# Moving the first expert tile's transposes and first product into the last attention step of a gated-linear-attention and mixture-of-experts kernel

## The chip, the core and the metric

The kernel runs on one core of one Trainium2 chip. The metric is the device time of one execution in microseconds (us), and the times given for a kernel are the median of several executions. The engines are named as in the profile: PE (TensorE, with PEld its weight loads), DVE (VectorE), ACT (ScalarE), POOL (GpSimd) and SP (SyncE, which here only issues transfers).

## The reference, cut to what matters

```python
# attention block; x is (8, 512, 256), two heads of 128 channels
h = layernorm(x)
q, k, v = silu(h @ wq), sigmoid(h @ wk), h @ wv
f = 1 - k                                  # decay of each channel
theta = cumsum(sign(f - 0.5)) * pi         # so cos is +-1, sin is 0
S = S * f + k (x) v ; o = (q * scale) . S  # a scan over 512 tokens
o = layernorm(o * sigmoid(h @ wg1 @ wg2)) * norm_w
x1 = x + o @ wo
# expert block on z = layernorm(x1); 8 experts, 4096 rows
e = argmax(z @ centroids.T) ; alpha = sigmoid(max affinity)
y = z + relu(layernorm(z, ln_g[e], ln_b[e]) @ w1[e].T + b1[e]) @ w2[e].T + b2[e]
out = x1 + alpha * y + (1 - alpha) * z     # rows in their old order
```

## The kernel before

**Attention as a pipeline.** Eight sequences (NSEQ) go through nine steps (`pipeline`, `step(a, b, c, nxt)`). In step i sequence a is projected, b, the one before it, has its scan, and c, two before, has its gated output normed, projected with `wo`, added to x and routed. The order of the instructions on each engine is written out by hand in that engine's `step`. Engines meet by counting semaphores: `need(eng, sem, per, s, k)` makes an engine wait until event k of sequence or tile s has happened. In the last step (i = 8) a is None, b is the last sequence (LAST_SEQ) and c the one before it (LAST_BUT_ONE).

**The scan.** It is a tree of seven levels over each chunk of 128 tokens. For a level and a head, ACT copies the keys that take part (`mix`), PE multiplies them with the queries (`level`, line 978, into one of two banks bank_l), DVE multiplies the decays in (`update`, line 1328) and picks the scores (`pick`, line 1339). The next level waits for these. Behind level 6 come `k_transposes` (line 1043), copies of them by ACT (`k_tok_copies`), `key_values` (line 1056), a short chain on DVE (`states`, lines 1511 and 1519) and `outputs` (lines 1070 and 1071). `output` on DVE gates the result (`gating`, line 1530).

**Routing.** `ranks` (PE) and `slots` (DVE) give each row a place in its expert's region of a DRAM buffer, `scatter_rows` (POOL, line 631) writes the rows there, each with z, x1 + z, alpha and its row number. The tables of the first NA = 12 tiles need only the first five sequences (EARLY); they are made in step 7 (`early_tables`, signals s_idx 1 and 2). The tables of the others are made behind sequence 7 (`last_tables`, s_idx 3 to 5).

**Expert tiles.** 39 tiles of 128 rows, each of one expert. For tile n: POOL fetches its rows (`gather`, line 683) into one of four slots (SLOTS) and SP the expert's w1 of 1 MB (`fetch_w1`, line 531) into one of four; PE transposes the 256 channels (`z_transposes`, line 1203, into bank_b[0]); ACT applies the expert's norm gains (`gains`, line 911, into xl_t, of which there are two); PE makes the first product (`up`, line 1215, 32 matmul records in two banks bank_a); DVE adds b1 (`bias_h`, line 1627); ACT takes the relu (`relu`, line 921); PE makes the second product (`down`, line 1231); DVE finishes (`finish`, lines 1636 and 1641); POOL scatters to the output (`scatter`, line 695). On PE `turn(n)` is up(n+1), z_transposes(n+2), down(n). Tiles from 12 on use `down_in_parts`, and most are in a loop (`rounds`).

**Around the change.** Behind the last step PE does z_transposes 0 and 1, the ranks of sequence 6 (LAST_BUT_ONE), up(0), the transposes of the last sequence's output (line 1087), then turn(0), the projection with wo (line 1094), turn(1), and so on, with the parts of the last sequence's end between turns. On SP the first four w1 fetches come behind the last step's fetch of x_res, which waits for `residual` (DVE, line 1505) of the sequence before. On POOL the four first gathers stand in the last step behind `norm("o", c)` and one `scatter_rows`. The arena is one block of SBUF that both halves of the kernel lay out anew; xl_t and y_sb lie over the level masks, which the last sequence's picks still read.

## Time and profile before

| | |
|---|---|
| median of 3 runs | 609.88 us |
| the three runs | 609.61, 609.88, 614.47 us |
| profiled execution | 613.98 us, its span 612.2 us |
| PE busy | 568.2 us (93% of the span) |
| PE weight loads busy | 490.3 us (80%) |
| DVE, ACT, POOL busy | 432.9, 341.8, 313.1 us |
| mean granted PE clock | 0.982 of full speed |

The span is the time from the first to the last instruction of the profiled execution; 1.8 us lie around it. Busy shares are averages over stages whose limits differ, so a change of one stage is read in that stage's rows. Matmuls are pipelined: a record may begin before the one ahead of it has ended, and the step from one group's start to the next one's is what a group costs.

### The profile page before, as it was taken

How to read it: one execution, taken by the hardware profiler on the slowest of the kernel's cores; microseconds unless marked ns; L12 is line 12 of the kernel's file. 1: busy time of each engine (PE TensorE's matmuls, PEld its weight loads, DVE VectorE, ACT ScalarE, POOL GpSimd, SP SyncE). 2: the span in 40 equal slices, each digit the busy share in tenths (PEclk: the TensorE clock that was granted, in tenths of full speed). 3: DMA queues.
4: the chain of work that ended last, by engine and by line, in shares of the span. 5: the costliest groups of instructions: out<-in, count | busy, mean ns of one | idle time of the engine just before them, and what ended most of it. 6: DMA issues, size and time to landing. Idle time of an engine off the chain costs nothing.

```text
span 612.2 us, 12947 instructions
## 1 busy us (share of the span) xinstructions
PE 568.2 (93%) x3854; PEld 490.3 (80%) x3854; DVE 432.9 (71%) x990; ACT 341.8 (56%) x754; POOL 313.1 (51%) x390
## 2 busy tenths in 40 slices
PE   2988999999999999999779999999999999999991
PEld 1556778687777867777669998999999999999990
DVE  1396895969779597898672445435888888888880
ACT  3464758768586775856564342224565565565550
POOL 7715244564725548253613425335767767767721
PEclk9999999999999999999699999999999999999996
DMA  8920111121112011020469447556765665665400
GB/s 300 417 94 0 35 36 35 70 70 60 46 35 76 30 69 36 13 92 2 124 213 347 168 160 256 190 190 208 231 217 193 225 228 190 239 224 195 142 6 0
DMA packets 25188, 83.61 MB, mean 137 GB/s; under 512 B 3821, under 2 KB 13423, under 8 KB 18992
## 3 DMA queue, kind: packets, MB, share of 16 engines
q1 hardware_dynamic: 16896, 59.57, 27.6%
q0 software_dynamic: 7552, 22.89, 11.4%
q8 instruction: 24, 0.39, 0.3%
q10 hardware_dynamic: 688, 0.52, 0.3%
q14 instruction: 28, 0.23, 0.1%
HBM read 70.35 MB, written 13.53 MB: 137 GB/s over the span
## 4 chain that ended last, share of the span: by engine, by line
PE 81%; DVE 8%; issue 4%; POOL 3%; DMA 2%; ACT 1%; DVEq 0%; ACTq 0%; POOLq 0%
PE bank_a L1215 21%; PE bank_a L990 8%; PE bank_l L978 7%; PE bank_l L1231 6%; PE bank_l L1250 4%; PE bank_l L1245 4%; PE bank_l L1246 4%; PE bank_c L1094 4%; PE bank_a L1019 4%; DVE arena L1328 3%; PE bank_b L1071 3%; PE bank_a L1035 2%; PE bank_a L1028 2%; PE bank_b L1070 2%; PE bank_c L1111 2%
## 5 line engine op out<-in xcount | busy, mean ns | idle before, releaser
L1215 PE MATMUL bank_a<-masks,arena 128*128 128x128 f32 x1248 | 145.9, 275 | 0.0
L1215 PEld LDWEIGHTS bank_a<-masks,arena 128*128 128x128 f32 x1248 | 143.4, 192 | 0.5
L1328 DVE TENSOR_TENSOR arena<-arena 128x256 f32<-128x256 f32 x224 | 92.1, 456 | 12.4 <-PE bank_l L978 11.0
L978 PEld LDWEIGHTS bank_l<-arena,k_mix 128*128 128x128 f32 x448 | 65.2, 197 | 43.7 <-ACT k_mix L732 27.4
L1627 DVE TENSOR_TENSOR arena<-bank_a,b_col 128x512 f32<-128x512 f32 x78 | 53.9, 691 | 63.9 <-PE bank_a L1215 52.7
L683 POOL DMA_INDIRECT arena<-rows_by_expert,take_idx x39 | 47.7, 1223 | 81.7 <-DVE k_mix L1641 79.3
L978 PE MATMUL bank_l<-arena,k_mix 128*128 128x128 f32 x448 | 72.9, 288 | 10.6 <-DVE arena L1339 7.3
L990 PE MATMUL bank_a<-arena 128*128 128x512 f32 x160 | 82.0, 611 | 0.0
L732 ACT ACTIVATE k_mix<-arena 128x128 f32<-128x128 f32 x224 | 60.4, 308 | 35.7 <-DVE arena L1328 30.7
L911 ACT ACTIVATE masks<-bank_b,b_col,g_col 128x128 f32<-128x128 f32 x78 | 31.4, 454 | 60.4 <-PE bank_b L1203 60.4
L1647 DVE TENSOR_TENSOR w_low<-w_sb,w_high 128x2048 fp32r<-128x2048 f32 x27 | 61.9, 2293 | 3.7 <-issue 2.8
L689 POOL TENSOR_SCALAR put_of<-arena,skip 128x1 int32<-128x1 f32 x39 | 61.7, 1583 | 1.0
L921 ACT ACTIVATE h_high<-arena 128x512 fp32r<-128x512 f32 x54 | 31.1, 623 | 53.8 <-PE bank_l L1250 51.2
L657 POOL TENSOR_TENSOR arena<-arena 128x512 f32<-128x512 f32 (+6 forms) x56 | 27.5, 490 | 59.4 <-DVE arena L1489 55.6
L695 POOL DMA_INDIRECT out<-k_mix,put_of x39 | 41.4, 1063 | 24.2 <-DVE k_mix L1641 13.5
L1245 PE MATMUL bank_l<-w_high,h_high 128*128 128x256 f32 x216 | 53.0, 288 | 0.8 <-ACT h_high L921 0.8
L732 ACT ACTIVATE w_high<-w_sb 128x2048 fp32r x27 | 51.2, 1895 | 0.0
L1246 PE MATMUL bank_l<-w_low,h_high 128*128 128x256 f32 x216 | 50.6, 277 | 0.0
L1231 PE MATMUL bank_l<-w_sb,arena 128*128 x192 | 43.7, 381 | 1.3 <-issue 1.3
L732 ACT ACTIVATE arena<-bank_a 128x512 f32<-128x512 f32 x40 | 23.8, 594 | 34.5 <-PE bank_a L1019 28.5
L631 POOL DMA_INDIRECT rows_by_expert<-arena x32 | 33.5, 1048 | 16.6 <-issue 16.6
L1245 PEld LDWEIGHTS bank_l<-w_high,h_high 128*128 128x128 f32 x216 | 40.6, 188 | 1.0 <-issue 1.0
(160 smaller groups left out, 1079.4 us busy)
## 6 DMA issues: line engine op xcount, KB each, us to landing
arena<-w SPq DMA_DIRECT2D x39, 1024.0 KB
arena<-x SPq DMA_DIRECT2D x16, 512.0 KB, 3.5
w_sb<-w SPq DMA_DIRECT2D x8, 1024.0 KB, 14.8
arena<-b SPq DMA_DIRECT2D x1, 1024.0 KB
arena<-rows_by_expert,take_idx POOLq DMA_INDIRECT x39
out<-k_mix,put_of POOLq DMA_INDIRECT x39
rows_by_expert<-arena POOLq DMA_INDIRECT x32
arena<-wk SPq DMA_DIRECT2D x1, 256.0 KB, 4.0
```

The source lines that it names most:

```text
L683: pool.indirect_dma_start(out=gathered[p].bitcast(I32), out_offset=None, in_=rows, in_offset=bass.IndirectOffsetOnAxis(ap=take_idx[:, n:n ...
L689: pool.tensor_scalar(put_of[:, n:n + 1], gathered[p][:, 2 * D + 1:2 * D + 2], skip[:, n:n + 1], None, ALU.add).then_inc(s_put, 1)
L732: return act.activation(dst, src, ACT.Copy)
L978: ins = pe.matmul(bank, k_mix[l % 2][:, m * P:(m + 1) * P], level_queries(buf, m, l), start=True, stop=True)
L990: return pe.matmul(bank[:, :], w[:, i * width + h * P:i * width + (h + 1) * P], xn_t[:, i * T:(i + 1) * T], start=(i == 0), stop=(i == DC ...
L1215: m = pe.matmul(bank_a[k // 4][:, k % 4 * P:(k % 4 + 1) * P], w1_now[t.par][:, i * F + k * P:i * F + (k + 1) * P], xl_t[t.par % 2][:, i * ...
L1231: m = pe.matmul(bank_l[p][:, 0:D], h_act[:, k * P:(k + 1) * P], w2_sb[:, bass.ds(e * (FC * D) + k * D, D)], start=(k == 0), stop=(k == FC ...
L1245: pe.matmul(bank_l[p][:, 0:D], h_high[:, h], w2_high[p][:, w], start=(k == 0), stop=False)
L1246: pe.matmul(bank_l[p][:, 0:D], h_high[:, h], w2_low[p][:, w], start=False, stop=False)
L1328: dve.tensor_tensor(half, half, factor(decay[b.par], h, l, second), ALU.mult).then_inc(s_up, 1)
L1627: dve.tensor_tensor(h_sb[:, n * 512:(n + 1) * 512].rearrange("p (k t) -> p k t", t=P), bank_a[n][:, :].rearrange("p (k t) -> p k t", t=P), ...
L1647: dve.tensor_tensor(w2_low[t.par % 2], w2_of(e), w2_high[t.par % 2], ALU.subtract).then_inc(s_wlo, 1)
```

## The change

Four moves, each with what has to go with it.

1. z_transposes(0) goes into the last step of PE, behind level 3 and the output transposes of c; up(0) follows in the same step, its first half ahead of `k_transposes`, its second half between these and `key_values`. ACT's gains(0) stands behind o_copy, ahead of mix 5, its relu(0) behind x1_copies; DVE's bias_h(0) stands behind `states`. xl_t[0] moves from the masks to a place of its own in the arena.
2. Behind the last step the order of PE becomes z_transposes(1), down(0), ranks, up(1), z_transposes(2), output transposes, turn(1), projection, turn(2) and so on: the parts of the last sequence stand one turn later. ACT, DVE and POOL follow.
3. SP fetches w1 of tile 0 at the start of the last step, then waits for the rows of all four first tiles, then fetches w1 of tiles 1 to 3 and b2; the fetch of x_res comes behind these.
4. POOL's gathers 0 and 1 stand at the head of the last step, 2 and 3 where they all stood; turn(0) comes ahead of `double_norm(LAST_SEQ)`.

```diff
--- before.py
+++ after.py
@@ -182,6 +182,7 @@
...
         gathered = [lay3.take(RW + 2)[:, 0:RW] for _ in range(SLOTS)]
+        xl_0 = lay3.take(DC * P)
         h_sb = lay3.take(F)
@@ -223,8 +224,8 @@
...
         over_masks = masks[:, :].bitcast(F32)
-        xl_t = [over_masks[:, i * DC * P:(i + 1) * DC * P] for i in range(2)]
-        y_sb = over_masks[:, 2 * DC * P:2 * DC * P + D]
+        xl_t = [xl_0, over_masks[:, 0:DC * P]]
+        y_sb = over_masks[:, DC * P:DC * P + D]
         norm_col = sb("norm_col", [P, DC], F32)
@@ -508,10 +509,6 @@
...
                     sp.dma_start(tiles(x_sb[ahead.par]), seq_rows(x_t, ahead)).then_inc(s_x[ahead.par], 16)
-                if b is not None:
-
-                    need_apart(sp, s_x1, 2, b, 0)
-                    sp.dma_start(tiles(x_res), seq_rows(x_t, b)).then_inc(s_xres, 16)
                 if a is None:
@@ -519,8 +516,16 @@
...
                     need(sp, s_q0, 1, b, 1)
-                    for n in range(SLOTS):
+                    fetch_w1(tile(0))
+                    for p in range(SLOTS):
+                        sp.wait_ge(s_rows[p], 16)
+                    for n in range(1, SLOTS):
                         fetch_w1(tile(n))
+                    sp.dma_start(b2_sb, b2.rearrange("e f -> (e f)").partition_broadcast(P)).then_inc(s_b2, 16)
+                if b is not None:
+
+                    need_apart(sp, s_x1, 2, b, 0)
+                    sp.dma_start(tiles(x_res), seq_rows(x_t, b)).then_inc(s_xres, 16)
 
@@ -531,10 +536,9 @@
...
-
-            sp.dma_start(b2_sb, b2.rearrange("e f -> (e f)").partition_broadcast(P)).then_inc(s_b2, 16)
             for n in range(SLOTS, NA):
                 fetch_w1(tile(n))
+            sp.wait_ge(s_idx, 3)
             rounds(sp, fetch_w1)
@@ -632,18 +636,22 @@
...
             def step(a, b, c, nxt):
+                if a is None:
+
+                    pool.wait_ge(s_idx, 2)
+                    need(pool, s_o, 2, c, 2)
+                    need(pool, s_og, 2, c, 2)
+                    need(pool, s_state, 5, c, 5)
+                    pool.wait_ge(s_row_out[0], 16 * TJ * EARLY)
+                    for n in range(2):
+                        gather(n)
                 if c is not None and b is not None:
...
-
-                    pool.wait_ge(s_idx, 2)
-                    need(pool, s_o, 2, c, 2)
-                    need(pool, s_state, 5, c, 5)
-                    pool.wait_ge(s_row_out[0], 16 * TJ * EARLY)
-                    for n in range(SLOTS):
+                    for n in range(2, SLOTS):
                         gather(n)
@@ -707,11 +715,12 @@
...
             scatter_rows(LAST_BUT_ONE)
+            turn(0)
             double_norm(LAST_SEQ)
-            for n in range(4):
+            for n in range(1, 5):
                 turn(n)
             scatter_rows(LAST_SEQ)
-            for n in range(4, NA - SLOTS):
+            for n in range(5, NA - SLOTS):
                 turn(n)
@@ -880,6 +889,9 @@
...
                 of(a, one_minus_k, 1)
+                if a is None:
+                    act.wait_ge(s_small, 64)
+                    gains(tile(0))
                 for l in (5, 6):
@@ -893,6 +905,8 @@
...
                 of(a, gate_sigmoid, 1)
+                if a is None:
+                    relu(tile(0))
 
@@ -939,25 +953,23 @@
...
 
-            act.wait_ge(s_small, 64)
             act.sem_inc(s_whi, 1 + NA)
             need(act, s_pick, 2 * MASKED, LAST_SEQ, 2 * MASKED)
-            gains(tile(0))
             gains(tile(1))
...
                 o_norm(LAST_SEQ, j)
-            relu(tile(0))
+            gains(tile(2))
+            relu(tile(1))
             for i in range(DC):
                 o_copy(LAST_SEQ, i)
-            gains(tile(2))
-            turn(tile(1))
-            relu(tile(2))
+            gains(tile(3))
+            turn(tile(2))
             x1_copies(LAST_SEQ)
-            gains(tile(4))
+            turn(tile(3))
             rows_of(LAST_SEQ)
-            turn(tile(3))
+            turn(tile(4))
             alphas(LAST_SEQ)
-            for n in range(4, NA):
+            for n in range(5, NA):
                 turn(tile(n))
@@ -1159,6 +1171,9 @@
...
                 of(c, o_transposes, 1)
+                if a is None:
+                    need(pe, s_og, 2, c, 2)
+                    z_transposes(tile(0))
                 of(b, level, 4, 0)
@@ -1171,12 +1186,17 @@
...
                 of(a, q_proj, 1, 1)
+                if a is None:
+                    need(pe, s_at0, H, b, H)
+                    up(tile(0), range(FC // 2))
                 if b is None:
...
                 of(a, g1_proj, 1)
+                if a is None:
+                    up(tile(0), range(FC // 2, FC))
                 of(b, key_values)
@@ -1203,11 +1223,11 @@
...
 
-            def up(t):
+            def up(t, ks=range(FC)):
 
...
                 pe.wait_ge(s_w1[t.par], t.half * 16 + 16)
-                for k in range(FC):
+                for k in ks:
                     if k % 4 == 0:
@@ -1267,29 +1287,29 @@
...
             c = LAST_SEQ
-            need(pe, s_og, 2, c, 2)
-            z_transposes(tile(0))
+            need(pe, s_og, 2, c, 1)
             z_transposes(tile(1))
-            ranks(LAST_BUT_ONE)
-            need(pe, s_at0, H, c, H)
-            up(tile(0))
-            o_transposes(c, 0)
-            o_transposes(c, 1)
             pe.wait_ge(s_w2, 16 * E)
...
             need(pe, s_wide, 6, c, 6)
-            turn(tile(0))
+            down(tile(0))
+            ranks(LAST_BUT_ONE)
+            up(tile(1))
+            z_transposes(tile(2))
+            o_transposes(c, 0)
+            o_transposes(c, 1)
+            turn(tile(1))
             for half in range(2):
...
                     out_proj(c, half, j)
-            turn(tile(1))
+            turn(tile(2))
             x1_transposes(c)
-            turn(tile(2))
+            turn(tile(3))
             for n in range(DC * TJ):
                 affinity(c, n)
-            turn(tile(3))
+            turn(tile(4))
             ranks(c)
-            for n in range(4, NA):
+            for n in range(5, NA):
                 turn(tile(n))
@@ -1529,6 +1549,20 @@
...
+
+            def bias_h(t, n):
+                if isinstance(t.half, int) and n == 0:
+                    dve.wait_ge(s_idx, 1 if number(t) < NA else 3)
+                e = dve.value_load(expert_of(t), min_val=0, max_val=E - 1)
+
+                need(dve, s_hr, 2, t, 0)
+                if in_parts(t):
+                    need(dve, s_hlo, 2, before(t, 1), n + 1)
+                need(dve, s_h, 2, t, n + 1)
+                b = b1_col[:, bass.ds(e * FC + n * FC // 2, FC // 2)]
+                dve.tensor_tensor(h_sb[:, n * 512:(n + 1) * 512].rearrange("p (k t) -> p k t", t=P),
+                                  bank_a[n][:, :].rearrange("p (k t) -> p k t", t=P),
+                                  b.unsqueeze(2).broadcast_to([P, FC // 2, P]), ALU.add).then_inc(s_hb, 1)
 
@@ -1585,6 +1619,8 @@
...
                     states(b)
+                    for n in range(2):
+                        bias_h(tile(0), n)
                     output(b, c)
@@ -1613,20 +1649,6 @@
...
-
-            def bias_h(t, n):
-                if isinstance(t.half, int) and n == 0:
-                    dve.wait_ge(s_idx, 1 if number(t) < NA else 3)
-                e = dve.value_load(expert_of(t), min_val=0, max_val=E - 1)
-
-                need(dve, s_hr, 2, t, 0)
-                if in_parts(t):
-                    need(dve, s_hlo, 2, before(t, 1), n + 1)
-                need(dve, s_h, 2, t, n + 1)
-                b = b1_col[:, bass.ds(e * FC + n * FC // 2, FC // 2)]
-                dve.tensor_tensor(h_sb[:, n * 512:(n + 1) * 512].rearrange("p (k t) -> p k t", t=P),
-                                  bank_a[n][:, :].rearrange("p (k t) -> p k t", t=P),
-                                  b.unsqueeze(2).broadcast_to([P, FC // 2, P]), ALU.add).then_inc(s_hb, 1)
 
@@ -1678,25 +1700,28 @@
...
             slots(LAST_BUT_ONE)
+            bias_h(tile(1), 0)
+            dve.wait_ge(s_b2, 16)
+            need(dve, s_pick, 2 * MASKED, c, 2 * MASKED)
+            finish(tile(0))
+            bias_h(tile(1), 1)
             for n in range(2):
-                bias_h(tile(0), n)
-            turn(tile(0))
+                bias_h(tile(2), n)
             for half in range(2):
...
             moments("u", c)
-            dve.wait_ge(s_b2, 16)
-            turn(tile(1))
             turn(tile(2))
+            turn(tile(3))
             affinities(c)
             route(c)
-            turn(tile(3))
+            turn(tile(4))
             slots(c)
             for part in range(3):
-                turn(tile(4 + part))
+                turn(tile(5 + part))
                 last_tables(part)
-            for n in range(7, NA):
+            for n in range(8, NA):
                 turn(tile(n))
...
             finish(tile(TILES - 1))
```

The function `bias_h` is only moved ahead of `step`, unchanged.

## Rows read from the trace of the kernel before

**Rows 1.** The profile's page: its head, and the chain by engine.

```profile
span 612.2 us, 12947 instructions
...
PE 81%; DVE 8%; issue 4%; POOL 3%; DMA 2%; ACT 1%; DVEq 0%; ACTq 0%; POOLq 0%
```

**Rows 2.** Windows: stretch, its length, busy time (and count) by engine, PE clock, DMA.

```profile
320.00:360.00 40.00, 38.89 (x281) 36.63 (x280) 16.37 (x47) 17.46 (x38) 14.22 (x23) 1.00 0.69 240
360.00:600.00 240.00, 235.72 (x1945) 230.75 (x1943) 177.99 (x252) 115.52 (x163) 144.49 (x110) 1.00 0.57 193
```

**Rows 3.** Timeline of PE, last step and junction: start, duration, group, idle before, releaser.

```profile
297.71 1.92 PE L1087 MATMUL bank_c<-ident,arena 128*128 128x128 f32 x8
299.42 1.40 PE L978 MATMUL bank_l<-arena,k_mix 128*128 128x128 f32 x8
...
301.99 0.68 PE L978 MATMUL bank_l<-arena,k_mix 128*128 128x128 f32 x4 [0.30 <-DVE arena L1339]
...
309.04 0.88 PE L1043 MATMUL bank_b<-ident,arena 128*128 128x128 f32 x6 [0.85 <-DVE arena L1328]
310.70 1.58 PE L1056 MATMUL bank_b<-arena 128*128 128x128 f32 x12 [0.78 <-ACT arena L732]
...
313.82 0.46 PE L1071 MATMUL bank_b<-arena 128*128 128x128 f32 x2 [0.67 <-DVE arena L1519]
...
319.75 0.44 PE L1203 MATMUL bank_b<-ident,arena 128*128 128x128 f32 x2 [0.79 <-DVE arena L1530]
321.30 0.41 PE L1203 MATMUL bank_b<-ident,arena 128*128 128x128 f32 x2 [1.11 <-ACT masks L911]
```

**Rows 4.** The chain in order of time, junction to turn(0): start, share of it, group.

```profile
320.51 0.30 ACTq L907
...
322.08 3.65 PE bank_a L1215 x32
325.74 1.04 PE bank_c L1087 x8
326.78 3.57 PE bank_a L1215 x32
...
330.57 3.46 PE bank_l L1231 x16
```

**Rows 5.** Timeline of ACT, last step.

```profile
299.70 0.58 ACT L732 ACTIVATE arena<-bank_c 128x512 f32<-128x512 f32 x1
300.93 0.59 ACT L732 ACTIVATE k_mix<-arena 128x128 f32<-128x128 f32 x2 [0.65 <-issue]
...
315.54 0.60 ACT L849 ACTIVATE arena<-arena,u_shift,u_rstd 128x256 f32<-128x256 f32 x1 [1.65 <-POOL u_shift L615]
```

**Rows 6.** Timeline of DVE, last step: the chained part of `states`.

```profile
312.43 1.25 DVE L1519 SCALAR_TENSOR_TENSOR arena<-arena,bank_b 128x128 f32<-128x128 f32 x4
```

**Rows 7.** Timeline of POOL, last step: a norm, the last of four gathers.

```profile
290.65 0.28 POOL L595 TENSOR_SCALAR o_neg_mean<-o_mom 128x4 f32<-128x4 f32 x1 [10.54 <-issue]
...
303.86 0.95 POOL L683 DMA_INDIRECT arena<-rows_by_expert,take_idx  x1 [0.30 <-issue]
```

**Rows 8.** Line 1328 in 299 to 309 us: shortest/median/longest ns, first and last start.

```profile
L1328 DVE TENSOR_TENSOR arena<-arena x13: 413/420/426, 298.8 to 308.6; 128x256 f32<-128x256 f32 x13
```

**Rows 9.** The whole chain in order of time: a gather it passes through.

```profile
376.37 6.04 DMA arena<-rows_by_expert,take_idx
```

**Rows 10.** Timeline of PE behind the junction, tiles 8 and 6.

```profile
382.46 0.44 PE L1203 MATMUL bank_b<-ident,arena 128*128 128x128 f32 x2 [0.50 <-DMA arena<-rows_by_expert,take_idx]
383.31 3.72 PE L1231 MATMUL bank_l<-w_sb,arena 128*128 x16 [0.41 <-issue]
```

**Rows 11.** Windows of 1 us each, columns as in Rows 2: where the PE clock falls and returns.

```profile
289.00:290.00 1.00, 0.72 (x4) 0.52 (x4) 1.00 (x4) 0.65 (x3) 0.00 (x0) 0.95 0.00 0
290.00:291.00 1.00, 0.91 (x4) 0.91 (x4) 1.00 (x7) 0.10 (x2) 0.28 (x1) 0.50 0.02 8
...
300.00:301.00 1.00, 1.00 (x9) 0.97 (x8) 0.58 (x2) 0.35 (x2) 0.96 (x1) 0.93 0.68 263
```

## The prediction

> **What bounds the kernel now.** I began with the page's head and the chain that ended last [rows 1]: PE holds 81% of a span of 612.2 us, so time comes off only where PE waits, or where work is put into its waits. The windows by stage [rows 2] say where that can be: from 320 to 360 us PE is busy 38.89 of 40 us, from 360 to 600 us 235.72 of 240. Behind the junction between attention and experts nearly all is PE's own work, so what is won ahead of it stays won, and no more than about 4 us is to be had behind it. Ahead of it stands the last step, with no projections to fill the waits between levels. PE's timeline there [rows 3] shows what the change aims at: idle 0.85 us before the key transposes (for DVE's last decay), 0.78 before the key products (for ACT's copies), 0.67 before the outputs (for DVE's states); then 0.79 before z_transposes(0) (for the gate of the last sequence) and 1.11 before z_transposes(1) (for gains(0)). The chain in order of time [rows 4] prices the rest: up(0) 3.65, output transposes 1.04, up(1) 3.57, down(0) 3.46.
>
> **Move 1, into the last step: what it costs there.** z_transposes(0) is two records. At the junction they took 0.44 [rows 3]. Behind the output transposes PE goes straight on to level 4 [rows 3], so they are paid in full: 0.44 if the clock there is as low as in this execution, half of that if not. Their rows must be there by 297.71 + 1.7 = 299.4; gather 0, below, starts at about 288, and the slowest gather that the chain shows took 6.04 [rows 9], so they land by 294 or 295, with 4 us to spare. On ACT gains(0) is 0.30 of register loading [rows 4] and two ACTIVATEs, which took 0.81 at the junction. It stands behind o_copy, which ends at 299.70 + 0.58 = 300.28 [rows 5], so ACT is free at 301.4 and mix 5, which began at 300.93 [rows 5], is 0.46 late. Level 5 waited in fact for DVE's pick until 301.99 [rows 3], while that mix ended at 301.52; so all but 0 to 0.1 of it is hidden. Sum for the levels: 0.5, between 0.2 (full clock, gains hidden) and 0.9 (nothing hidden).
>
> up(0) is half of 3.57 in each half, 1.79. The last level ends at about 308.2, late by 0.5: 308.7. Then first half 1.79, key transposes 0.7 (0.88 less the overlap of its last record), second half 1.79, during which ACT makes its copies: the key products start at 313.0 instead of 310.70 [rows 3], 2.3 later. So 3.57 of work cost 1.8 besides the 0.5; the two idle times of 0.85 and 0.78 hide the rest. Behind the key products DVE was still busy with the last moments until 312.0 and began its states then; when the products come later it is free, and the first of them are there about 1.0 after their start. States were 0.39 for a copy and 1.25 for the chained part [rows 6] and with the signals 1.8, so the outputs start at 313.0 + 1.0 + 1.8 = 315.8 or 315.9 instead of 313.82 [rows 3]: **2.1 later**. DVE's bias_h(0), two instructions of 0.69 with a register load ahead of each, stands in the 3.2 us in which DVE waited for the outputs; it costs nothing there. ACT's relu(0) (1.15) waits for it until about 317.5, and rows_of, which began at 315.54 [rows 5], begins at about 318.7. It needs 4 us and alphas 0.3, so gains(1) can start at 323.0. That is the tightest follow-on: up(1) wants its result at 325.
>
> **Move 2, the junction.** Outputs end at 319.0 + 2.1 = 321.1. z_transposes(1) needs only the first half's gate, long done: no idle. down(0) follows with relu(0) done at 318.7: 3.46. Ranks about 0.4, then up(1) at 325.2, for which gains(1) is ready at 324.2. Gone from this place are the idle 0.79, the 0.45 of z_transposes(0), the idle 1.11 and up(0) with 3.65: **6.0**. What is late next: between z_transposes(2) and up(2) only the output transposes (1.04) are left to hide gains(2), which needs 0.81 and two signals of about 0.15: up(2) may wait 0.1 to 0.2. I take 0.2, between 0 and 0.5. The output transposes need POOL's norm and ACT's four passes, at 328, and stand at 329: hidden.
>
> **Move 3, SP.** fetch_w1(0) is issued at about 287.2, when the gate of c is written, and has 20 us until up(0). Behind it SP waits for four gathers; the last was issued at 303.86 [rows 7], its rows are there by 310. Queued behind this wait are w1 of tiles 1 to 3, b2 and x_res. up(1) wants w1 at 325, finish(0) b2 at 328, the last residual x_res at 341, so the wait and the order cost nothing; w1 of tile 4 can even go out at 313, since up(0) is done by then. If the cover were gone, each us of lateness of w1(1) beyond 15 us would count.
>
> **Move 4, POOL.** Gathers 0 and 1 start at 287.1 plus a signal and are issued by 290.4 to 290.9, if each costs as much as the 0.95 and the gap of 0.30 of a later one [rows 7]. Behind them is the norm that began at 290.65 [rows 7]; it is 0 to 0.25 late, and ACT's o_norm has about 0.5 to spare: nothing. The two stand beside DVE's level 0, whose instructions have two SBUF inputs. In the stretch with the four gathers of before, line 1328 kept to 413 to 426 ns [rows 8], so the one doesn't hold up the other here. The Trainium skill speaks against this move: by SBUF — State Buffer, Who interferes with whom, a DVE instruction with two SBUF inputs and a GpSimd instruction that reads SBUF hold each other up for whole instructions. Last, turn(0) ahead of the double norm sends gather 4 out at 332 instead of 343. Gather 9 takes the place of gather 8 behind the last scatter_rows; gather 8 cost PE 0.50 and 0.41 [rows 10], and I take gather 9 to cost the same. An earlier one (tile 7) cost about as much again; its place gets looser by the ranks, another's tighter. I put these at 0, within 0.9 either way.
>
> **The sum.** 6.0 off at the junction, less 2.1 and 0.2: 3.7. Profiled, 612.2 - 3.7 = 608.5 for the span and 610.3 for the execution. The median of before is 609.88 and its profiled execution 613.98, so the same 3.7 makes 606.2 of the median. Bounds from the terms alone: levels 0.3 less or 0.4 more, gains(2) 0.2 less or 0.3 more, gathers 0.9 either way, gives 604.8 to 607.8.
>
> **Rivals.** (a) **The hidden part is not hidden**: if PE's idle before the key products only moves, because k_tok copies or the states end later than I reckon, or ACT's longer queue (relu(0) before rows_of) makes gains(1) later than 325, the gain is only the junction's idle, 0.79 + 1.11 = 1.9, less 0.5 for the levels: 608.5. For it: three engines meet at short distances there. Against it: each has over 1 us of slack by the sum above.
>
> (b) **The upper of two times.** One of the three runs took 614.47, and the profiled one 613.98, 4.1 above the median. The granted PE clock falls from 1.00 to 0.50 (from 2.4 to 1.2 GHz) at 289.9 and is back at 300.1 [rows 11], behind the waits of levels 0 and 1. The eight records of the output transposes took 1.92 there and 1.04 at full clock [rows 3, 4]; with the levels' products that makes 2 to 3 us, most of the 4.1. So executions probably differ in whether the clock falls, and nothing ahead of 297 changes for PE. If the median of after is of the upper kind: 606.2 + 4.2 = 610.4, level with before.
>
> (c) **Slower: the clock falls again in the step's tail.** If up(0) no longer meets a full clock but a half one (or a fall comes later, because the levels end later), PE's work of 10.2 us at half clock costs 5.1: 606.2 + 5.1 = 611.3. It decides from about 3.7 us of cost, that is 7.4 us of busy PE at half clock. Against it: after 300.1 the clock stayed at 1.00 through all idle times up to 321, and the change makes PE busier there. The Trainium skill (TensorE: Matmul & The Clock Gate, What's actually happening) has the half clock as the state of rest, which activity lifts; the row agrees.
>
> (d) **The shared port rule holds after all**: each early gather then holds DVE's level 0 for about its 0.95, 1.9 in all, straight in the chain: 608.1. The same page of the Trainium skill is its ground; rows 8 speak against it.
>
> (e) The change does more: the gathers' waits behind 365 fall away too, 1.8 us: 604.4.
>
> **How the numbers follow.** Forecast 606.2: 0.62. (a) 0.13, (b) 0.13, (c) 0.04, (d) 0.03, (e) 0.05. The range is 604.5 to 610.0: it holds the forecast with its bounds, (a) and (d) and a part of (b). A change of 1% (6.1 us) is about what a measurement of this kernel can tell from none. Faster by over 1% (below 603.8) needs all of (e) and a cheap last step, 0.05; slower (above 616.0) needs (b) and (c) together, 0.02; within 1% is 0.93.
>
> **What would show it.** Right: in PE's timeline z_transposes(0) behind the output transposes without idle; both idle times around the key transposes gone; outputs start about 2.1 later; no idle before z_transposes(1); up(1) follows the ranks at once; the projection with wo starts at about 337.5. Wrong: idle before level 4 or 5 with gains or a gather as the releaser, before up(1) or up(2) with line 911, or before down(0) with line 921; more waits on gathers between 340 and 420; a second stretch at clock 0.50.

## The result, and the profile after

Ten executions of each kernel: before 611.39 us (609.09 to 614.88), after 608.42 us (606.33 to 610.77). The ratio is **0.9944** (95% interval 0.9922 to 0.9966): 3.4 us less, between 2.1 and 4.8 (the two medians as they stand differ by 3.0). The forecast was 3.7 less. The level of before itself came out 1.5 us above the median of three that the prediction started from, so the times themselves are higher: after came to 608.42 where 606.2 was forecast, inside the range of 604.5 to 610.0.

The profiled execution of after took 607.61, 6.4 less than that of before. That is more than the comparison of many executions gives, so the two first traces can't be subtracted as a whole: 2.4 of it (286.19 against 283.82) lie ahead of level 0 of the last step, where the change moves nothing. The pages' heads, as in [rows 1]:

```profile
span 605.9 us, 12951 instructions
...
PE 84%; DVE 6%; issue 3%; POOL 3%; DMA 2%; ACT 1%; DVEq 0%; POOLq 0%; ACTq 0%
```

PE now holds 84% of the chain instead of 81%. The timeline of PE in after, last step and junction; lines 990, 1055, 1068, 1083, 1099, 1223, 1235 and 1251 are 978, 1043, 1056, 1071, 1087, 1203, 1215 and 1231 of before:

```profile
283.82 1.07 PE L990 MATMUL bank_l<-arena,k_mix 128*128 128x128 f32 x8
...
295.35 1.91 PE L1099 MATMUL bank_c<-ident,arena 128*128 128x128 f32 x8
297.05 0.56 PE L1223 MATMUL bank_b<-ident,arena 128*128 128x128 f32 x2
297.45 1.06 PE L990 MATMUL bank_l<-arena,k_mix 128*128 128x128 f32 x8
...
299.67 0.68 PE L990 MATMUL bank_l<-arena,k_mix 128*128 128x128 f32 x4 [0.30 <-DVE arena L1359]
...
303.68 0.61 PE L990 MATMUL bank_l<-arena,k_mix 128*128 128x128 f32 x4
304.12 1.95 PE L1235 MATMUL bank_a<-arena 128*128 128x128 f32 x16
305.91 0.82 PE L1055 MATMUL bank_b<-ident,arena 128*128 128x128 f32 x6
306.56 1.95 PE L1235 MATMUL bank_a<-arena 128*128 128x128 f32 x16
308.35 1.50 PE L1068 MATMUL bank_b<-arena 128*128 128x128 f32 x12
...
311.30 0.46 PE L1083 MATMUL bank_b<-arena 128*128 128x128 f32 x2 [0.57 <-DVE arena L1539]
...
316.31 0.38 PE L1223 MATMUL bank_b<-ident,arena 128*128 128x128 f32 x2
316.53 3.62 PE L1251 MATMUL bank_l<-w_sb,arena 128*128 x16
...
320.35 3.82 PE L1235 MATMUL bank_a<-masks,arena 128*128 128x128 f32 x32
...
324.23 1.04 PE L1099 MATMUL bank_c<-ident,arena 128*128 128x128 f32 x8
325.41 3.84 PE L1235 MATMUL bank_a<-arena 128*128 128x128 f32 x32
...
336.21 3.73 PE L1235 MATMUL bank_a<-masks,arena 128*128 128x128 f32 x32
```

Square brackets mark PE's waits, and few are left. Of the five waits of [rows 3] that the prediction named, 0.85, 0.78, 0.79 and 1.11 us are gone, and the 0.67 before the outputs is 0.57. z_transposes(0) costs 0.40 (297.05 to 297.45). up(0) stands in two halves of 1.79 around the key transposes. Behind the outputs come z_transposes(1) and down(0) without a wait. Before up(2), PE lost 0.3 us to the late gains(2), which end at 325.36 on ACT: the output transposes took 0.87 from start to start in the second trace of before (322.65 to 323.52), and here 1.18 lie between 324.23 and 325.41.

Further on there is something new. The same timeline, tiles 6 to 9, and below it the windows of 1 us where the clock falls (columns as in [rows 11]):

```profile
361.19 3.82 PE L1235 MATMUL bank_a<-arena 128*128 128x128 f32 x32
...
375.77 3.73 PE L1235 MATMUL bank_a<-arena 128*128 128x128 f32 x32
381.97 0.44 PE L1223 MATMUL bank_b<-ident,arena 128*128 128x128 f32 x2 [2.47 <-DMA arena<-rows_by_expert,take_idx]
382.82 5.35 PE L1251 MATMUL bank_l<-w_sb,arena 128*128 x16 [0.42 <-issue]
388.01 3.73 PE L1235 MATMUL bank_a<-masks,arena 128*128 128x128 f32 x32
```

```profile
382.00:383.00 1.00, 0.58 (x3) 0.35 (x4) 0.87 (x5) 0.43 (x2) 0.98 (x2) 0.87 1.01 385
383.00:384.00 1.00, 1.00 (x3) 0.82 (x4) 0.19 (x1) 0.37 (x2) 0.26 (x1) 0.50 1.00 389
```

PE waits 2.47 us for the rows of tile 9 and 0.42 for a register load behind them; then the granted clock is 0.50 (1.2 GHz), and down(7) takes 5.19 (382.82 to 388.01) instead of 3.45: 1.74 more. The two waits and the half clock make 4.6 us. The waits of before were 0.19, 0.68, 0.50 and 0.41, together 1.8, on tiles 7 and 8 [rows 10 has the last two]. The waits in brackets leave something out, though, and from start to start the difference is smaller. These are the same products in the first trace of before, behind the end of the projection and down(1) (344.56):

```profile
344.56 1.04 PE L1103 MATMUL bank_c<-ident,arena 128*128 128x128 f32 x8
...
362.30 3.82 PE L1215 MATMUL bank_a<-masks,arena 128*128 128x128 f32 x32
...
378.22 3.73 PE L1215 MATMUL bank_a<-masks,arena 128*128 128x128 f32 x32
...
386.86 3.73 PE L1215 MATMUL bank_a<-masks,arena 128*128 128x128 f32 x32
```

The three turns behind the ranks took before 24.56 us (362.30 to 386.86) and after 26.82 (361.19 to 388.01); in the second traces of both, taken later, it is 24.10 (359.21 to 383.31) and 26.78 (360.16 to 386.94). So after loses **2.3 to 2.7 us more** here. On POOL the gather of tile 9 (line 691) stands behind the block of four row transfers (line 635, in 369.75 to 374.58):

```profile
373.62 0.96 POOL L635 DMA_INDIRECT rows_by_expert<-arena  x1 [0.31 <-issue]
374.62 0.34 POOL L697 TENSOR_SCALAR put_of<-arena,skip 128x1 int32<-128x1 f32 x1
375.24 1.06 POOL L691 DMA_INDIRECT arena<-rows_by_expert,take_idx  x1 [0.28 <-POOL put_of L697]
```

It was issued 0.53 us ahead of up(8) (375.77). In before, gather 8 behind the same block was issued at 376.37 [rows 9], 1.85 ahead of up(7), which began at 378.22.

### The profile page after: what moved, and what is told of

Same layout as the page of the kernel before. It is cut to its first block, busy times and chain, and to the rows that moved or that the text cites. A ratio compares the mean times of both kernels' runs of the same rounds, so it can differ in the third digit from the quotient of the medians.

```text
span 605.9 us, 12951 instructions
## 1 busy us (share of the span) xinstructions
PE 567.7 (94%) x3854; PEld 492.4 (81%) x3854; DVE 434.5 (72%) x990; ACT 340.7 (56%) x754; POOL 312.5 (52%) x390
## 4 chain that ended last, share of the span: by engine, by line
PE 84%; DVE 6%; issue 3%; POOL 3%; DMA 2%; ACT 1%; DVEq 0%; POOLq 0%; ACTq 0%
PE bank_a L1235 22%; PE bank_a L1002 10%; PE bank_l L990 7%; PE bank_l L1251 6%; PE bank_c L1106 4%; PE bank_l L1270 4%; PE bank_l L1265 4%; PE bank_l L1266 4%; PE bank_a L1031 4%; PE bank_b L1083 3%; PE bank_a L1047 2%; PE bank_a L1040 2%; PE bank_b L1082 2%; PE bank_c L1123 2%; PE bank_b L1068 2%
## 5 line engine op out<-in xcount | busy, mean ns | idle before, releaser
L1348 DVE TENSOR_TENSOR arena<-arena 128x256 f32<-128x256 f32 x224 | 93.9, 465 | 7.6 <-PE bank_l L990 7.5
L691 POOL DMA_INDIRECT arena<-rows_by_expert,take_idx x39 | 47.7, 1223 | 87.1 <-DVE k_mix L1663 76.9
L1235 PE MATMUL bank_a<-arena 128*128 128x128 f32 x640 | 75.1, 275 | 0.1
L1235 PEld LDWEIGHTS bank_a<-arena 128*128 128x128 f32 x640 | 73.5, 192 | 0.5 <-ACT arena L925 0.4
L1235 PE MATMUL bank_a<-masks,arena 128*128 128x128 f32 x608 | 71.1, 275 | 0.0
L1235 PEld LDWEIGHTS bank_a<-masks,arena 128*128 128x128 f32 x608 | 69.9, 192 | 0.3
L703 POOL DMA_INDIRECT out<-k_mix,put_of x39 | 41.6, 1068 | 24.1 <-DVE k_mix L1663 13.4
L1251 PE MATMUL bank_l<-w_sb,arena 128*128 x192 | 45.2, 390 | 0.4 <-issue 0.4
L635 POOL DMA_INDIRECT rows_by_expert<-arena x32 | 33.8, 1055 | 16.6 <-issue 16.6
```

The costliest lines, as they stand in the source:

```text
L691: pool.indirect_dma_start(out=gathered[p].bitcast(I32), out_offset=None, in_=rows, in_offset=bass.IndirectOffsetOnAxis(ap=take_idx[:, n:n ...
L1235: m = pe.matmul(bank_a[k // 4][:, k % 4 * P:(k % 4 + 1) * P], w1_now[t.par][:, i * F + k * P:i * F + (k + 1) * P], xl_t[t.par % 2][:, i * ...
L1251: m = pe.matmul(bank_l[p][:, 0:D], h_act[:, k * P:(k + 1) * P], w2_sb[:, bass.ds(e * (FC * D) + k * D, D)], start=(k == 0), stop=(k == FC ...
L1348: dve.tensor_tensor(half, half, factor(decay[b.par], h, l, second), ALU.mult).then_inc(s_up, 1)
```

## The experiments

Ten runs in three rounds, two of them the kernels before and after once more. Each was timed beside before on the same chip; the ratio is to before.

**Before and after once more.** No edit.

> The kernel before, once more, for a second trace of it. In the first one DVE waited 2.11 us before its decay at level 5 (304.62), which the trace after does not show (0.20). Theory A, the wait is a chance of that execution: here the stretch from the first product of level 0 in the last step to the first record of line 1071 is 26 us or less instead of 27.6, the wait at level 5 is under 0.6, and the change then costs the step about the 2.1 forecast. Theory B, it belongs to the order of before: the wait of some 2 us stands at the same place again, and the stretch is 27.6 within 0.3. Time against before: ratio 1.000 within 0.004.

> The kernel after, once more, beside the others on one chip. Time 3 to 4 us under before (ratio 0.994 within 0.003). In its trace the wait for the rows of tile 9 (2.47 us in the first one, then 1.7 us of half clock) stands again if it comes from the order on POOL and the traffic there (theory A: 1 us or more); it is under 0.6, as in the trace of before, if it was a chance (theory B).

Measured: before again 611.08 us, 1.0001 (0.998 to 1.0023); after again 607.29, **0.9944** (0.9917 to 0.9972). The second trace of before, timeline of PE:

```profile
283.43 1.07 PE L978 MATMUL bank_l<-arena,k_mix 128*128 128x128 f32 x8
...
303.04 0.61 PE L978 MATMUL bank_l<-arena,k_mix 128*128 128x128 f32 x4
304.50 0.88 PE L1043 MATMUL bank_b<-ident,arena 128*128 128x128 f32 x6 [0.85 <-DVE arena L1328]
306.16 1.58 PE L1056 MATMUL bank_b<-arena 128*128 128x128 f32 x12 [0.78 <-ACT arena L732]
...
309.28 0.46 PE L1071 MATMUL bank_b<-arena 128*128 128x128 f32 x2 [0.67 <-DVE arena L1519]
...
317.37 5.45 PE L1215 MATMUL bank_a<-masks,arena 128*128 128x128 f32 x32
322.65 1.04 PE L1087 MATMUL bank_c<-ident,arena 128*128 128x128 f32 x8
...
341.47 1.04 PE L1103 MATMUL bank_c<-ident,arena 128*128 128x128 f32 x8
```

From level 0 to the outputs there are 25.85 us, not the 27.63 of the first trace: the wait of 2 us at level 5 was a chance of that execution, and theory A holds. The outputs of after come at 27.48 and in its second trace at 27.86, so **1.6 to 2.0 later** than in a clean before. But this before has a loss of its own: up(0) takes 5.28 (317.37 to 322.65) instead of 3.65, at half clock. After again waited 2.38 us for tile 9 and had 1.8 of half clock behind it, as in its first trace: theory A there too.

**The transposes alone.** To before were added: the space for xl_t[0], the changes of SP, the early gathers 0 and 1, gains(0) and z_transposes(0) in the last step. up(0) and all behind it stay at the junction.

```diff
+                if a is None:
+                    need(pe, s_og, 2, c, 2)
+                    z_transposes(tile(0))
                 of(b, level, 4, 0)
...
-            need(pe, s_og, 2, c, 2)
-            z_transposes(tile(0))
+            need(pe, s_og, 2, c, 1)
             z_transposes(tile(1))
             ranks(LAST_BUT_ONE)
             need(pe, s_at0, H, c, H)
             up(tile(0))
```

> Before, with a part of the change: gathers 0 and 1 and w1 of tile 0 early, z_transposes(0) and gains(0) in the last step; up(0) and all behind it stays at the junction. Theory A (up(0) is hidden by half in the last step, 3.65 of work for 1.6 to 1.8 of delay): this kernel gains only the junction's waits, 0.79 and 1.11, less 0.4 for the transposes in the step, so 1.4 us under before, and the full change is 2 us or more faster than it. Rival (the waits at the key transposes are not filled, up(0) only changes place): this kernel is as fast as the full change, within 0.7 us.

Measured: 611.72 us, **1.0004** (0.9977 to 1.0031). The full change was 3.7 us faster than this one (0.9944 against 1.0004), more than the 2 us that theory A asked for at least; but the 1.4 us under before that A gave this kernel are not there, and the rival is out. Its timeline of PE at the junction says why:

```profile
315.58 0.38 PE L1215 MATMUL bank_b<-ident,arena 128*128 128x128 f32 x2
317.59 0.41 PE L1131 MATMUL bank_c<-arena 128*128 128x32 f32 x2 [1.63 <-DVE arena L1394]
```

The waits of 0.79 and 1.11 are gone, and the ranks behind them wait 1.63 us for DVE's route. So I tried the ranks further back (DVE's slots of that sequence go between its two bias_h of tile 0 with them):

```diff
             z_transposes(tile(1))
-            ranks(LAST_BUT_ONE)
             need(pe, s_at0, H, c, H)
             up(tile(0))
+            ranks(LAST_BUT_ONE)
```

> The kernel with the transposes only, and with the ranks of sequence 6 behind up(0) instead of ahead of it (DVE's slots go between its two bias_h of tile 0). The transposes alone won nothing (1.0004): behind z_transposes(1) PE waited 1.63 us for DVE's route, which those ranks need. Theory A (that wait took the place of the two removed ones, and the change as a whole escapes it since its ranks stand behind down(0)): the wait is gone and the kernel is 1.2 to 1.8 us under before; what the full change has over it is then up(0) in the step's waits, about 2 us. Rival (something else eats the gain): within 0.6 us of before.

Measured: 610.84 us, 0.999 (0.9966 to 1.0015): within 0.6 us of before, as the rival has it. The interval reaches from 2.1 us under before to 0.9 over it and doesn't exclude A's 1.2 to 1.8 by itself; its trace says where they went:

```profile
321.86 0.39 PE L1132 MATMUL bank_c<-arena,ones 128*128 128x32 f32 x2
323.75 0.73 PE L1096 MATMUL bank_c<-ident,arena 128*128 128x128 f32 x2 [1.50 <-ACT arena L767]
```

The ranks wait no more, as A had it, but the output transposes behind them now wait 1.50 us, and 0.16 twice, for ACT's norm of the last sequence. That norm hangs on a chain that begins at the last outputs: gate and moments on DVE, norm on POOL, four passes on ACT. PE reaches the transposes sooner and gets nothing for it. What the change as a whole does is to put down(0) and up(1), over 7 us, in front of those transposes, with up(0) already done.

**The last rows in two halves.** On POOL two of the four transfers go behind turn(4), two behind turn(5), once in after and, a turn earlier, once in before.

```diff
-            scatter_rows(LAST_SEQ)
-            for n in range(5, NA - SLOTS):
+            scatter_rows(LAST_SEQ, range(2))
+            turn(5)
+            scatter_rows(LAST_SEQ, range(2, TJ))
+            for n in range(6, NA - SLOTS):
                 turn(n)
```

> After, with the last scatter of rows on POOL in two halves, two transfers behind turn(4) and two behind turn(5), so that gather 9 goes out on time. Theory A (the block of four transfers sends gather 9 late, and its wait of 2.47 us, 0.42 of register load and 1.7 of half clock follow from that): gather 9 starts about 2 us earlier, its wait is under 0.6 and the time is 2 to 4 us under after. Rival (the wait comes from the traffic of w1 and rows, not from the issue): wait and time within 0.7 us of after.

> Before, with the last scatter of rows on POOL in two halves (behind turn(3) and turn(4)). Before waits 0.5 to 0.6 us for the rows of tile 8, with 0.41 of register load behind it, and once 0.19 and 0.68 for tile 7. Theory A (after lost 2.9 us more on this block than before did): the split is worth about 1 us here, where it was worth 3.5 us in the kernel after (0.9885 against 0.9944). Rival (the split is worth as much on either kernel, so the change did not make the block dearer): 3 us or more here.

Measured: after with the split 604.39 us, **0.9885** (0.9851 to 0.9919), so 3.6 us under after (0.9885 / 0.9944 = 0.9941). Before with the split 608.93 us, 0.9977 (0.9955 to 0.9999), 1.4 us. Theory A on both: before's interval (0.1 to 2.7 us) shuts out the 3 us of the rival. POOL in after with the split, and below it PE:

```profile
375.19 1.06 POOL L692 DMA_INDIRECT arena<-rows_by_expert,take_idx  x1 [0.63 <-POOL put_of L698]
```

```profile
377.68 3.73 PE L1238 MATMUL bank_a<-arena 128*128 128x128 f32 x32
381.25 0.38 PE L1226 MATMUL bank_b<-ident,arena 128*128 128x128 f32 x2
382.13 3.72 PE L1254 MATMUL bank_l<-w_sb,arena 128*128 x16 [0.51 <-issue]
```

Gather 9 is issued 2.49 ahead of up(8) instead of 0.53, there is no wait for its rows, and the down product behind it takes its usual time. The three turns behind the ranks now take 22.59 us (363.10 to 385.69) instead of 26.8, and in before with the split 23.24 instead of 24.1 to 24.6. By the timed runs the block cost before 1.4 us and after 3.6.

**Dummies in before's junction.** Six and eight transposes of the identity into a free bank, around z_transposes(0).

```diff
+            need(pe, s_wide, 6, c, 6)
+            fill(6)
             need(pe, s_og, 2, c, 2)
             z_transposes(tile(0))
+            fill(8)
             z_transposes(tile(1))
```

> Before, with 6 and 8 dummy transposes of the identity (0.11 us each, into a bank that is free) in PE's two waits at the junction. They leave the waits as long and only keep PE busy. In the second trace of before the clock was at 0.50 from 317.4 to about 321 and up(0) took 5.28 instead of 3.65; in the first it was not. Theory A (the clock falls behind the junction's waits in most executions, and the change gains by not having them): 0.5 to 1.8 us under before. Rival (it is rare, or dummies of so few us don't hold the clock): within 0.4 us of before.

Measured: 610.18 us, 1.0002 (0.9973 to 1.0031). No gain, and an interval of 1.8 us to either side: theory A isn't shown. The one trace of it has no fall of the clock behind the junction, and its span, 606.6, is the shortest of all that keep up(0) there; but it then waits 1.21 us for the rows of tile 8, more than the 0.50 of [rows 10].

**Dummies in the last step.** In after, transposes of the identity behind levels 0, 1 and 2; then the same with the rows in two halves.

```diff
                 of(b, level, 0, 1)
+                if a is None:
+                    need(pe, s_og, 2, c, 2)
+                    fill(8)
...
                 of(b, level, 1, 1)
+                if a is None:
+                    fill(12)
...
                 of(b, level, 2, 1)
+                if a is None:
+                    fill(12)
```

> After, with dummy transposes of the identity on PE in the waits of the last step: 8 behind level 0, 12 behind level 1, 12 behind level 2 (3.5 us of work in waits of 0.9 and 1.3 us or more, in a bank that is free). In all six traces so far the clock is at 0.50 for about 10 us from level 1 on. Theory A (the waits let it fall, work in them holds it): the clock stays at 1.00, the levels' eight records take 1.1 instead of 2.05, the output transposes 1.0 instead of 1.9, and the kernel is 2 to 3 us under after. Rival (the levels are bound by DVE and ACT, or the clock falls in spite of it): within 0.7 us of after, or above it if the dummies stand in the way.

> After, with both the dummy transposes in the last step and the last scatter of rows in two halves. If the two are independent the gains add: 3.5 us of the split and the 2 to 3 us that theory A gives the fill, 6 us under after and 9 to 10 under before. If the fill is worth nothing, as the split alone, 0.9885 of before. If an earlier step only makes PE come sooner to a gather that is late, the sum is less than the two.

Measured: 606.12 us, **0.9921** (0.9895 to 0.9946), and with the split 604.16 us, **0.9874** (0.9841 to 0.9907). The fill is worth 1.4 us on after and 0.7 on after with the split, each within the error of the comparison, and the 1.4 short of the 2 to 3 of theory A; the sum is less than the two expected, the last case that was named. Timeline of PE in after with the fill:

```profile
289.55 1.54 PE L990 MATMUL bank_l<-arena,k_mix 128*128 128x128 f32 x8 [0.43 <-DVE arena L1370]
290.93 1.47 PE L1051 MATMUL bank_b<-ident 128*128 128x128 f32 x12
292.41 1.54 PE L990 MATMUL bank_l<-arena,k_mix 128*128 128x128 f32 x8
293.79 1.04 PE L1103 MATMUL bank_c<-ident,arena 128*128 128x128 f32 x8
```

The output transposes take 1.04 and not 1.91: full clock. The clock was at 1.00 in all windows from 280 to 330 us, and the outputs begin 25.93 us behind level 0 where the two traces of after have 27.48 and 27.86. So 1.6 to 1.9 us were won in the step. The 1.4 of the timed runs agrees with that within its error. This trace also had no fall of the clock behind the wait for tile 9, which was 1.03 us in it. In the trace with the split as well, part of the gain went here:

```profile
380.42 0.44 PE L1237 MATMUL bank_b<-ident,arena 128*128 128x128 f32 x2 [1.24 <-DMA arena<-rows_by_expert,take_idx]
```

**All of w1 first.**

```diff
-                    fetch_w1(tile(0))
-                    for p in range(SLOTS):
-                        sp.wait_ge(s_rows[p], 16)
-                    for n in range(1, SLOTS):
+                    for n in range(SLOTS):
                         fetch_w1(tile(n))
```

> After, with w1 of all four first tiles fetched at the start of the last step, ahead of the wait for the rows: 4 MB at some 400 GB/s are 10 us of traffic from 286 on, beside gather 0 whose rows z_transposes(0) wants 10 to 11 us behind its issue. Theory A (the rows come through between the packets of w1): no wait at z_transposes(0), within 0.7 us of after, so the order on SP that the change brings is worth nothing by itself. Rival (the rows queue behind the 4 MB): z_transposes(0) and with it levels 4 to 6 wait 1 us or more, and the kernel is 1 to 3 us over after.

Measured: 607.96 us, 0.9941 (0.9912 to 0.997), the ratio of after. Timeline of PE, and a window of the stretch in which w1 comes in:

```profile
296.91 0.38 PE L1220 MATMUL bank_b<-ident,arena 128*128 128x128 f32 x2
```

```profile
292.00:294.00 2.00, 0.71 (x4) 0.45 (x4) 2.00 (x5) 1.78 (x6) 1.26 (x2) 0.50 1.04 414
```

z_transposes(0) has no wait although 414 GB/s of w1 were on their way. Theory A: the order that the change gives SP is worth nothing measurable by itself in this place.

## Why the prediction was right

The gain, and how it comes about in the last step and at the junction, came out as forecast. That the total came so near is in part luck: one term was wrong, and something outside the sum made up for it. Measured on a clean pair (second trace of before, first of after), step by step:

- **z_transposes(0)** was put at 0.44 at half clock: level 4 begins 0.41 later against level 0 (13.63 against 13.22). **gains(0)** was put at 0 to 0.1 beside 0.46 of nominal delay; by level 5 the delay is 0.24 in all. The 0.5 taken for both was 0.25 here, and 0.6 in after's second trace, whose clock came back later.
- **up(0)** was put at 2.3 of delay for the key products and 2.1 for the outputs: 1.80 and 1.63 in this pair, 2.0 for the outputs in after's second trace. The two waits around the key transposes, which it was to fill, are gone. Rival (a) is refuted.
- **The junction** was put at 6.0 less 0.2. From the start of the outputs to the end of down(1) and the projection, before needs 32.19 (309.28 to 341.47), of which 1.63 are the half clock in up(0), so 30.6, and after 24.91 (311.30 to 336.21): **5.65**. With the first trace of before (313.82 to 344.56, 30.74) it is 5.83. The wait for gains(2) was 0.3.
- These make 5.65 - 1.8 = 3.85 with the mean delay of the two traces of after, for the 3.7 of the sum. The projection was to start at 337.5, 51.3 behind level 0; it starts 48.9 behind it (332.76). Of these 2.4 us, 1.8 are the chance wait at level 5 of the trace that the forecast was built on.
- **Move 3 and the early gathers of move 4** cost nothing, as said: z_transposes(0) found its rows even with 4 MB of w1 beside them. Rival (d), and with it the rule of the Trainium skill (SBUF — State Buffer, Who interferes with whom), holds nothing up here: line 1348 took 399 to 425 ns beside the two early gathers of after, and line 1328 413 to 426 in [rows 8]. That section itself reports a tensor_tensor that did not stall a DMA issued by POOL, so the rival read its rule more widely than it is meant.

One term was wrong: gather 9 "to cost the same" as gather 8, within 0.9. It and its neighbours cost **2.3 to 2.7 us more**, and so one of the signs named as wrong did appear: a longer wait on a gather between 340 and 420, with a further stretch at clock 0.50 behind it. The step that failed is that I compared the two blocks by their place on POOL alone. How late the rows are depends on PE too. In before the late rows of tile 7 had held PE for 0.19 + 0.68, and from up(5) to up(7) it took 15.92 us (362.30 to 378.22); after's PE had no such wait and took 14.58 (361.19 to 375.77) from up(6) to up(8). So it stood 1.3 us sooner before rows that were issued no sooner (14.05 behind that start, 14.07 in before) and took 0.6 longer to be there (6.73 against 6.09 from issue to use). Behind the waits of 2.47 and 2.38, and of 2.42 in the run with all of w1 first, the clock fell; behind waits of 0.50 to 1.24 at this place, in six other traces, it did not. The split shows that the place of the gather behind the block is the cause: it gives back 3.6 us in after and 1.4 in before.

With 3.85 won and 2.5 lost (the mean), 1.3 should be left, and 3.4 (2.1 to 4.8) were measured. Something that the sum didn't hold makes up 0.8 to 3.5 us. The first traces of both kernels and the second ones, cut at three records of PE, show where it lies (us):

| stretch | before | before again | after | after again |
|---|---|---|---|---|
| start to level 0 of the last step | 286.19 | 283.43 | 283.82 | 282.40 |
| to the end of the projection and down(1) | 58.37 | 58.04 | 52.39 | 52.77 |
| to the start of the first product of the last tile | 243.53 | 243.03 | 245.57 | 245.81 |
| to the end of the span | 24.1 | 24.1 | 24.1 | 24.1 |

The second stretch became 5.98 and 5.27 shorter, the third 2.04 and 2.78 longer: 3.9 and 2.5 in the two pairs, 3.2 in the mean, near the 3.4 measured. (The 2.4 and 1.0 of the first stretch are chance, since the change moves nothing there.) So the remainder is what before's own traces lost in the second stretch and the clean pair leaves out: 1.8 in the wait at level 5 in one, 1.6 at half clock in up(0) in the other. After had no such loss. The question left is whether before loses that much as a rule.

Other traces say that a loss there is common. The same stretch took 60.7 in before with the split and 59.7 in the transposes with late ranks; the two with neither a second fall nor a chance wait, the transposes alone and the filled junction, took 57.4 and 56.1. After, after again and after with the split took 52.4 to 52.8, and all of w1 first 53.7. What the slower ones lost is a second fall of the clock between 308 and 330 us in three of the six traces that have up(0) at the junction, and the wait at level 5 in the first. After has hardly a wait left there for a fall to begin behind, though it had one in one of four traces (all of w1 first, at 313). The mean granted clocks of the timed runs point the same way: over 89 runs of before they leave some 26.8 us of the span at half clock, over 22 of after 25.6 (an estimate that takes all that is missing from 1.00 as half clock), although after has 3.4 of these behind tile 9, where before's traces have none. They don't say where in the kernel the others lie, six traces are few, and filling the junction of before didn't make it measurably faster. So how often before has such a loss is **argued and not shown**, and the forecast owes the nearness of its total partly to two errors of opposite sign. Rival (b), that before's upper times come from the fall at 290, is refuted in its first part: that fall stands in every trace of before and after, whatever the time. Rival (c), a further fall in the step's tail, happened in both kernels, and in those like before more often.

The versions that beat both kernels are after with the rows in halves, 0.9885, and the same with dummies, 0.9874; the two can't be told apart.

## What to carry to other kernels

Work moved into another stage's waits pays what it fills, but look at what then stands first at the place that it left: both partial moves here won nothing that could be measured, since each removed wait had another of 1.5 to 1.6 us behind it, and only the move together with the new order paid. When an engine arrives sooner, recheck each transfer that it meets later by the distance between its issue and its use, not by its place in the queue; a block of four transfers of 1.3 us each in front of one that is needed at once is better cut in two.

## What the runs showed of the hardware

- The granted PE clock fell to 0.50 for about 7 to 10 us from level 1 or 2 of the last step on in all ten traces without the fill, though no wait of PE there was longer than 1.7 us. 32 dummy transposes of 0.11 us in the waits kept it at 1.00 there in both traces that had them. The Trainium skill (TensorE: Matmul & The Clock Gate, HAM oscillation — how this bites in real kernels) puts such a fall down to idle gaps of PE. The traces agree in that work put into the gaps kept the clock up; but no single gap here was long: they were short and many, with work between them.
- Where PE waited for a gather of 128 rows of 2 KB, it had taken 5.6 us from issue to use (before with the filled junction, 371.70 to 377.33), 6.7 (after) and 7.4 (after with fill and split, 372.97 to 380.42): one latency is no bound to plan by.
- A stream of w1 at 414 GB/s did not keep a gather issued beside it from being used 11.2 us behind its issue without a wait (all of w1 first, 285.74 to 296.91).
